# Attention with convolutions and a sphere convolution, one core: 28 instead of 20 row maxima taken in the first stage, four of them ahead of its last convolution, and one set of loads held back

## The reference

```python
x = x + attention(_gn(x), ...)        # _gn: group norm over 4 groups of channels
x = x + sphere_conv(_gn(x), weight, bias)

def attention(x, Wq, bq, q_conv_w, ...):
    q = _rope(split_heads(_conv(_mcl(x, Wq, bq), q_conv_w, q_conv_b, 3)))   # 8 heads of 32
    k = _rope(split_heads(_conv(_mcl(x, Wk, bk), k_conv_w, k_conv_b, 3)))
    v = split_heads(_conv(_mcl(x, Wv, bv), v_conv_w, v_conv_b, 3))
    qk = jnp.einsum('bceqd,bcekd->bceqk', q, k) / math.sqrt(h)
    a = jax.nn.softmax(qk, axis=-1)
    o = jnp.einsum('bceqk,bcekd->bceqd', a, v)
    return _conv(_mcl(o, Wo, bo), o_conv_w, o_conv_b, 0)
```

## Time and profile before

| | us |
|---|---|
| median of three runs | 1203.33 |
| profiled run | 1201.07 |
| its span in the profile | 1199.2 |
| TensorE busy | 1066.2 (89%) |
| VectorE busy | 818.5 (68%) |
| ScalarE busy | 712.1 (59%) |
| GpSimd busy | 766.4 (64%) |

### The profile page before, as it was taken

How to read it: one execution, slowest core, us unless ns; L and a number is a source line. 1 busy time by engine, 2 the same in 40 slices (tenths; PEclk the granted TensorE clock), 3 DMA queues, 4 the chain that set the end, 5 groups by cost and what they waited for, 6 DMA issues and landing times. The chain is left out here.

```text
span 1199.2 us, 25544 instructions
## 1 busy us (share of the span) xinstructions
PE 1066.2 (89%) x10352; PEld 565.7 (47%) x10352; DVE 818.5 (68%) x1174; ACT 712.1 (59%) x1164; POOL 766.4 (64%) x782
## 2 busy tenths in 40 slices
PE   0899999999987889998899999999877689799997
PEld 0777777777761233333333333333333245454553
DVE  5888665565557987888888888888841874444344
ACT  3877677777641665666676666666674332346345
POOL 1144545555451988998888889999895018919900
PEclk9999999999995998999999999999998899999999
DMA  9844343434348364271815454451000999775761
GB/s 307 298 133 132 108 111 94 137 100 112 102 121 196 51 155 90 59 119 39 129 47 102 74 92 89 78 100 46 11 19 30 300 347 297 243 233 160 199 198 48
DMA packets 137765, 159.05 MB, mean 133 GB/s; under 512 B 17856, under 2 KB 85712, under 8 KB 137644
## 3 DMA queue, kind: packets, MB, share of 16 engines
q1 hardware_dynamic: 114544, 122.58, 41.3%
q10 hardware_dynamic: 14560, 25.66, 6.2%
q0 software_dynamic: 8544, 9.18, 2.9%
HBM read 106.54 MB, written 52.89 MB: 133 GB/s over the span
## 5 line engine op out<-in xcount | busy, mean ns | idle before, releaser
L1250 POOL TENSOR_TENSOR a_pl<-a_prob 128x512 bf16<-128x512 f32 x416 | 442.3, 1092 | 42.3 <-ACT a_prob L1203 41.9
L1203 ACT ACTIVATE a_prob<-a_col 128x512 f32<-128x512 f32 x512 | 288.7, 596 | 154.7 <-PE a_col L1108 147.8
L1156 DVE TENSOR_REDUCE a_negmax<-a_row 128x1 f32<-128x512 f32 x384 | 246.5, 681 | 60.1 <-PE a_row L1087 59.1
L501 PE MATMUL f_acc<-f_wh,f_xhl 128*32 128x384 bf16 x2560 | 163.5, 327 | 0.0
L613 DVE TENSOR_TENSOR f_yl<-f_acc,f_yh 128x768 bf16<-128x768 f32 x80 | 76.3, 956 | 88.5 <-ACT f_yh L715 88.5
L1167 DVE TENSOR_TENSOR a_pl<-a_prob 128x512 bf16<-128x512 f32 x96 | 115.4, 1202 | 20.6 <-ACT a_prob L1203 20.6
L838 POOL TENSOR_TENSOR f_straight<-f_straight,f_turned 128x832 f32<-128x832 f32 x40 | 85.4, 2136 | 66.2 <-DVE f_turned L639 66.2
L1108 PE MATMUL a_col<-a_q,a_k 98*128 98x512 bf16 x256 | 97.8, 389 | 30.9 <-ACT a_prob L1203 26.9
L1108 PE MATMUL a_col<-q,k 98*128 98x512 bf16 x256 | 100.3, 392 | 25.8 <-ACT a_prob L1203 20.7
L1514 PE MATMUL b_acc_s<-b_xh,b_mat_h 128*104 128x512 bf16 x256 | 98.8, 386 | 12.1 <-DVE b_xl L1604 11.1
L501 PE MATMUL f_acc<-f_wl,f_xhl 128*32 128x384 bf16 x1280 | 107.7, 326 | 0.0
(11 more groups left out here) (174 smaller groups left out, 2063.4 us busy)
## 6 DMA issues: line engine op xcount, KB each, us to landing
X<-b_x ACTq DMA_DIRECT2D x16, 526.0 KB, 8.3
a_v<-V SPq DMA_DIRECT2D x16, 512.0 KB, 4.6
Z<-a_z ACTq DMA_DIRECT2D x32, 256.0 KB, 2.0
b_z<-Z SPq DMA_DIRECT2D x16, 512.0 KB, 10.9
b_x<-in_x SPq DMA_DIRECT2D x32, 256.0 KB, 10.3
b_res<-X SPq DMA_DIRECT2D x38, 208.0 KB
out<-b_y ACTq DMA_DIRECT2D x38, 208.0 KB
V<-f_vout SPq DMA_DIRECT2D x64, 104.0 KB
```

Source lines behind the costliest of these rows:

```text
L501: last = nc.tensor.matmul(acc[half][c * KW:(c + 1) * KW, part, 0:PART], xx[g % 2][:, (half * QUAD + c) * FH + f, at], ww[half * QUAD + c][ ...
L1156: nc.vector.reduce_max(negmax[n % PAIR][:, 0, t:t + 1], row[step % ROWS][:], AX.X, negate=True).then_inc(max_done, 1)
L1203: nc.scalar.activation(prob[sets_done % RING][:, t % QUAD, :], col[step % 2][:], ACT.Exp).then_inc(exp_done, 1)
L1250: nc.gpsimd.tensor_tensor(pl[p][:, r, :], prob[p][:, r, :], ph[p][:, r, :], ALU.subtract).then_inc(lo_pool, 1)
```

## The change

`EARLY` becomes 28, so `front` does 28 of unit 0's 32 row maxima, and `attend` leaves out 28 steps. In `front` the first four of them (as many as there are `acc` banks) move ahead: TensorE computes their score tiles ahead of the last convolution, behind a wait for the last `y_low` (the banks are free then), and VectorE takes their maxima ahead of the last turn's `rope_products`. The other 24 stay behind the last convolution. In `attend`, SyncE waits for `max_in[0]` (the rows of maxima of unit 0 have landed) ahead of `load_qk(0, 1, 0)`; everything behind it in SyncE's list waits with it.

```diff
-EARLY = 20
+EARLY = 28
@@ front, tensor
-            convolution(turn(TOTAL - 1))
-            for t in range(EARLY):
+            def early_row(t):
                 h, qt = t // (W // P), t % (W // P)
                 if t % (W // P * HALF) == 0:
                     pe.wait_ge(qk0_in[h // HALF], 16 * QK_LOADS)
...
                                  start=True, stop=True).then_inc(row_full, 1)
+
+            pe.wait_ge(yl_done, 2 * (turn(TOTAL - 1) + 1))
+            for t in range(len(row)):
+                early_row(t)
+            convolution(turn(TOTAL - 1))
+            for t in range(len(row), EARLY):
+                early_row(t)
@@ front, vector
+            def early_max(t):
+                v.wait_ge(row_full, t + 1)
+                nc.vector.reduce_max(negmax0[:, 0, t:t + 1], row[t % len(row)], AX.X, negate=True).then_inc(max_done, 1)
...
+                if n == TOTAL:
+                    for t in range(len(row)):
+                        early_max(t)
                 if n:
                     rope_products(n - 1)
...
-            for t in range(EARLY):
-                v.wait_ge(row_full, t + 1)
-                nc.vector.reduce_max(negmax0[:, 0, t:t + 1], row[t % len(row)], AX.X, negate=True).then_inc(max_done, 1)
+            for t in range(len(row), EARLY):
+                early_max(t)
             v.wait_ge(max_done, EARLY)
@@ attend, sync
             def load_qk(i, s, part):
+                if i == part == 0:
+                    sp.wait_ge(max_in[0], 16)
```

## The result

The changed kernel took 1191.3 us (median of 8 runs, 1186.4 to 1195.0), the kernel before 1201.84 us in the same comparison (8 runs, 1196.9 to 1204.6). The ratio is 0.991, with a 95% interval of 0.9888 to 0.9932: 10.5 us faster by the medians, 8 to 13.5 by the interval. In the profiled runs the span went from 1199.2 to 1190.4 us, and the start of the third stage from 930.83 to 921.75, 9.1 us earlier. Of all runs told of here one, the profiled run of e8, took 1279 us at a lower granted clock (0.84); it is in no comparison, and its profile isn't read.

A forecast was written before the change was run, and what follows sets the result against it. The first column product, bound by the DMA of maxima and VectorE's pace, comes 7.9 us earlier (385.94 to 369.05 + 9.0 = 378.05), with nothing given back: 1203.33 - 7.9 = 1195.4 us, range 1193.0 to 1199.3.

The forecast's parts named there:

- What bounds the seam: Between first and second stage: the first column product waits for the DMA of maxima and VectorE's pace; 7.9 us to gain.
- T: Start of the second stage's first column product on TensorE: 385.94 us before, forecast at 378.05, 7.9 us earlier.
- Four tiles and four maxima ahead, free: Before the last convolution and rope products: they fit idle gaps of 2.20 us (TensorE) and 4.87 us (VectorE), costing nothing.
- The clock: At the last convolution: with the gap cut to about 1.2 us the clock stays up, ending it 1.09 us earlier.
- End of the first stage: VectorE's maxima, not the stores, end last at 368.45 us; second stage starts at about 369.05, 0.15 us earlier.
- Eight maxima fewer in the second stage: At the second stage's start: 4.8 us less VectorE work; DMA of maxima issued 5.2 us in, instead of 10.01.
- The DMA of the maxima: Unit 0's, with SyncE's loads held behind it: takes 3.8 us instead of 6.7, landing 9.0 us into the second stage.
- The arbitration rule of the Trainium skill, as a rival: DMA engines alternate between queues, so unit 0's DMA of maxima still takes 6.7 us; gain 5.0 us, 1198.3 us; chance 0.1.
- The traffic meets unit 1: Rival: pushed-back loads delay unit 1's DMA of maxima, stall 1.9 us plus up to 2 us of clock; chance 0.1.
- The rows of units 2 and 3 come too late: Rival: held-back loads delay unit 2's first score tile; slower than before by 0.2% from 408 us on; chance 0.05.
- Nothing of it should be given back: Behind T: all engines stand at the same steps with the same lower clock, so the whole 7.9 us is kept.
- The zero point: Starting time of the sum: 1203.33 us for the kernel before, the median of runs, 2.26 us above the profiled run.

The follow-up runs named there:

- e8: Changed kernel plus a second SyncE wait, for unit 2's maxima, ahead of the two constants and unit 4's loads; ratio 0.9901 to the kernel before.
- e4: Changed kernel with all 28 score tiles and maxima behind the last convolution, none ahead; ratio 0.9937 to the kernel before.
- e2: Changed kernel without SyncE's wait for unit 0's maxima; 1203.44 us, ratio 1.0026 to the kernel before.
- e3: Kernel before with SyncE's wait for unit 0's maxima alone added; ratio 0.9936 to the kernel before.
- e7: Changed kernel with SyncE's wait moved behind the twelve part 0 loads, ahead of v of unit 2; ratio 1.001 to the kernel before.

## Why the prediction was right or wrong, point by point

**What bounds the seam: right.** T moved from 36.3 us behind the start of the last convolution (mean of two) to 28.0 (mean of three). The sum gave 7.9 us for that; it was 8.3. That T stood at 378.02 in the profiled run, where 378.05 was forecast, is partly luck: the first stage ran 0.8 us later in it than in the kernel before.

**Four tiles and four maxima ahead, free: right.** No engine waited for them, and beside e4 they save 2.40 us, VectorE's four maxima (4 x 0.598 = 2.39).

**The clock: right in the changed kernel, with a doubtful reason.** The q and k products took 2.30 us instead of 3.39, 1.09 less as computed. But e4 shows the gap of 2.20 us without the fall.

**End of the first stage: right.** VectorE was last; 19.22 us to the second stage against 19.47 computed (369.05 - 349.58). VectorE began its maxima 1.94 us behind the start of the rope products instead of 2.11, the change of stage took 0.51 us instead of 0.56, and the prediction's own sum, 368.45 + 0.56, is 369.01 and not 369.05.

**Eight maxima fewer in the second stage: right.** The DMA of the maxima went out 5.22 us into the stage, 5.2 computed.

**The DMA of the maxima: right in kind, a little mis-sized.** I took 3.8 us; it was 3.1, 3.6 and 3.7. T came 8.45 to 9.03 us into the stage, 9.0 computed. The price of the cover was judged wrongly all the same: I held the gain of the wait to be 2.9 us (6.7 - 3.8), the figure of the kernel before. In the changed kernel the wait shortens the DMA by 13.5 us (17.2 - 3.7), and without it the other parts make the kernel slower than before (e2). The 6.7 us were no property of the DMA but of its place between two groups of loads.

**The arbitration rule of the Trainium skill, as a rival: fell.** The rival said that holding loads back brings little; e2, e3 and e7 show that it decides the matter. In e2 both queues move packets, but only after a first phase in which ScalarE's queue moved nothing. The page "DMA: Bandwidth & Descriptors" of the Trainium skill has the turn-taking, packet by packet, in its section on arbitration. The trace doesn't agree with it for the first phase, and for the second only in that both queues move: 66 packets beside 940 are one in fifteen, not every other one.

**The traffic meets unit 1: it did, and cost nothing.** The transfers ended at 405 to 406 us and not at 403, so unit 1's DMA of maxima, issued at 402.95, stood behind them too. From 403 to 405 us only SyncE's queue moved, from 405 to 407 both:

```profile
q1 hardware_dynamic: 197, 0.26, 107.0%
```

```profile
q1 hardware_dynamic: 328, 0.17, 51.7%
q10 hardware_dynamic: 66, 0.02, 3.7%
```

Its last packet had moved by 406.4, and TensorE started the product at 407.82, behind a wait for ScalarE, as in the other two profiles of the changed kernel. So the cover held, but by no more than 1.4 us. The reason given for it, that the queue runs empty just then, was off by 3 us.

**The rows of units 2 and 3 come too late: it didn't happen.** No wait for a DMA shows at unit 2's first score tile in any of these profiles. (The list was late by 6.0 us for the twelve loads, 377.90 against 371.89, where the prediction says seven.)

**"Nothing of it should be given back", and nothing more gained: this step failed.** The sum let T alone move and left everything behind T as it was. Behind T the intervals were the same as before but for unit 2's: 36.24, 36.11 and 36.83 us instead of 37.38 and 37.87. I had seen its stall and took it to move along unchanged. The stall itself did, nearly (2.5 to 3.0 us of waiting against 2.8 and 3.6); what differs is how long the clock was low, 3.4 us instead of 6.8. I had put this as a risk on the slow side only. It is 1.2 us.

**The zero point: the other term that failed.** The sum starts from 1203.33 us, the median of three runs, 2.26 us above the profiled one. The median of eight was 1201.84, 0.8 above it (1200.46 of 29 in a later series). That is 1.5 us.

**The range: too narrow on the fast side.** The time came out 4.1 us below the forecast: 1.5 from the zero point, 0.4 from T, 1.2 from unit 2. That leaves 1.0 us which no interval of mine explains; the measurement's own interval is +-2.6 us, and I can't say whether it is anything. The zero point and T together would have left the time at 1193.5, inside the range; unit 2 takes it out. The runs scatter by 8 us within one kernel, and e4 shows one cause: where the clock falls in the tail, 2.9 us in a single place. I had allowed 1.5 us for all this, from three runs.

## What to carry to other kernels

A small DMA on which everything waits belongs ahead of the bulk loads, and a wait in the loading queue can put it there: first look for what is in flight when it is issued, then for what the loading queue may issue next. The time of such a DMA in a trace is that of its place among the loads, and a change of the order around it can more than double it (6.7 to 17.2 us), so it can't be carried over into the sum of another order, not even as an upper bound. Where one such stall is found, look for the others of the same kind: here a second wait took 3.2 us off the interval it stands in, and between 1 and 5 us off the time.

## What the runs showed of the hardware

A DMA of 16 KB on ScalarE's queue took 2.4 to 3.7 us with little in flight, 4.4 us behind two loads of v, 6.6 to 8.7, 14.4 and 17.2 us with twelve to twenty-four loads of 128 KB on SyncE's queue around it. In e2 and e7 it moved no packet until about 384 and 383 us, nine to ten microseconds behind its issue, whether loads were issued after it or not; its 66 packets then took 5 to 7 us, in e7 with the other queue nearly idle for the last half of them. In the changed kernel unit 1's DMA of maxima, issued at 402.95, moved none until 405 either, when the loads ahead of it were ending. I had expected a slowing by the traffic, and no time in which one queue stands still.

The same gap of 2.20 us of TensorE was followed by the lower clock in four profiles and not in a fifth, and the lower clock around unit 2's stall, 2.2 to 3.7 us long, lasted 3.4 us in seven profiles and 6.8 us in four. With two or three microseconds at stake each time, a kernel with such gaps is a few microseconds faster or slower from run to run with no change in its work.
